# One decoder layer with 16 long contexts: a rewritten start, row-tiled self-attention scores, a split query spread and a last pair of its own

## The reference

```python
x = x + self_attention(layernorm(x), wq, wk, wv, wo)         # 32 query heads, 8 key heads of width 16, causal
x = x + cross_attention(layernorm(x), ctx, Wq_d, W_qk, Wkv_d, Wv_u)
x = x + ffn(layernorm(x), gate, kernel, bias, lora_A, lora_B, lora_As, lora_Bs)

# cross_attention, 16 heads, latent width 32
C_kv = ctx @ Wkv_d                                   # 1500 x 32 for each sequence
q    = (layernorm(x) @ Wq_d) @ W_qk                  # 56 x 16 x 32
out  = softmax(q . C_kv / sqrt(32)) @ (C_kv @ Wv_u)
# ffn
A_eff, B_eff = gate @ lora_A, gate @ lora_B          # one pair of factors for every two sequences
out  = x @ kernel + bias + (x @ A_eff.T) @ B_eff.T + (x @ lora_As.T) @ lora_Bs.T
```

## Time and profile before

| | |
|---|---|
| median of the runs | 679.4 us |
| profiled execution | 681.57 us, of which the span of instructions is 679.6 us |
| TensorE (PE) busy | 591.6 us, 87% |
| VectorE (DVE) | 442.2 us, 65% |
| GpSimd (POOL) | 424.9 us, 63% |
| ScalarE (ACT) | 303.8 us, 45% |
| chain that ended last | PE 62%, DVE 12%, issue 7%, POOL 6%, ACT 5%, SP queue 3%, DMA 3% |
| stages | prologue 64.7, body 0 68.8, bodies 1 to 6 73.6 each in the mean, body 7 62, body 8 and the store 42 us |

### The profile page before, as it was taken

One profiled execution on the slowest core, in us unless ns is written; L12 is line 12 of the kernel. 1 busy time (PEld: TensorE's weight loads), 2 busy tenths in 40 slices (PEclk: granted clock), 3 DMA queues, 4 the chain that ended last, 5 costly groups with the idle time before them and its releaser, 6 DMA issues.

```text
span 679.6 us, 12918 instructions
## 1 busy us (share of the span) xinstructions
PE 591.6 (87%) x3856; PEld 306.8 (45%) x3856; DVE 442.2 (65%) x717; ACT 303.8 (45%) x641; POOL 424.9 (63%) x394
## 2 busy tenths in 40 slices
...
GB/s 310 211 210 245 236 119 18 78 210 166 43 29 228 211 44 1 115 323 57 17 42 271 154 43 31 225 215 43 1 130 333 32 15 47 43 9 1 22 1 14
DMA packets 31410, 77.22 MB, mean 114 GB/s; under 512 B 11378, under 2 KB 25042, under 8 KB 28915
## 3 DMA queue, kind: packets, MB, share of 16 engines
...
...
## 4 chain that ended last, share of the span: by engine, by line
PE 62%; DVE 12%; issue 7%; POOL 6%; ACT 5%; SPq 3%; DMA 3%; POOLq 0%; ACTq 0%; DVEq 0%
PE st_ps L649 11%; PE mx_ps L677 10%; PE pv_ps L664 9%; POOL acc L1096 5%; PE mi_ps L459 4%; PE mi_ps L466 4%; PE mi_ps L453 4%; PE mi_ps L512 4%; SPq L371 3%; PE mi_ps L631 2%; DVE mx_p L1020 2%; DVE sm L982 2%; PE mi_ps L537 2%; DMA b_eff<-acc 2%; PE mi_ps L635 2%
## 5 line engine op out<-in xcount | busy, mean ns | idle before, releaser
L1096 POOL TENSOR_TENSOR acc<-acc,p_ring 125x448 f32<-125x448 f32 x300 | 359.8, 1199 | 49.2 <-ACT p_ring L833 23.5
L1020 DVE TENSOR_REDUCE mx_p<-mx_ps 128x1 f32<-128x500 f32 x336 | 210.7, 669 | 101.7 <-PE mx_ps L677 100.6
L833 ACT ACTIVATE p_ring<-st_ps 125x448 f32<-125x448 f32 x384 | 189.7, 544 | 171.4 <-PE st_ps L649 164.4
L649 PE MATMUL st_ps<-q_st,c_st 98*125 98x448 f32 x384 | 155.3, 432 | 13.4 <-ACT p_ring L833 7.7
L677 PE MATMUL mx_ps<-c_st,q_st 96*128 96x500 f32 x336 | 139.4, 446 | 14.9 <-DMA q_st<-q_hl 11.2
L649 PEld LDWEIGHTS st_ps<-q_st,c_st 98*125 98x125 f32 x384 | 68.7, 191 | 117.1 <-ACT p_ring L833 88.2
L1104 POOL TENSOR_TENSOR rstd<-mv,eps_col 128x1 f32<-128x1 f32 x24 | 4.6, 192 | 153.2 <-DVE mv L894 153.2
L664 PE MATMUL pv_ps<-p_ring,c_nat 125*32 125x448 f32 x768 | 94.4, 564 | 1.0 <-ACT p_ring L833 0.9
L677 PEld LDWEIGHTS mx_ps<-c_st,q_st 96*128 96x128 f32 x336 | 63.2, 196 | 41.4 <-issue 20.6
L1096 POOL TENSOR_TENSOR acc<-p_ring 125x448 f32<-125x448 f32 x30 | 36.6, 1221 | 27.3 <-ACT p_ring L833 27.3
L466 PE MATMUL mi_ps<-ctx_sb,wkv_sb 128*32 128x375 f32 x512 | 48.1, 496 | 0.7 <-DVE p L943 0.7
...
## 6 DMA issues: line engine op xcount, KB each, us to landing
...
```

The source lines that it names most:

```text
L649: mm(st_ps[unit % STB][0:KC, 0:HALF], c_st[:, b % 4, t * KT + k * KC:t * KT + (k + 1) * KC], q_st[:, b // 2 % 2, b % 2, half * HALF:(half ...
L833: act.activation(p_ring[:, unit % PR, :], st_ps[unit % STB][0:KC, 0:HALF], ACT.Exp, scale=float(L) ** -0.5).then_inc(exp_done, 1)
L1020: ve.tensor_reduce(mx_p[:, p:p + 1], mx_ps[unit % MXB][:, 0:KP], AX.X, ALU.max).then_inc(red_done, 1)
L1096: po.tensor_tensor(dst, first, p_ring[:, unit % PR, :].rearrange("p (h s) -> p h s", s=S), ALU.add).then_inc(acc_done, 1)
```

## The change

Five parts in one.

1. Prologue. The host pads `x` to 64 rows, so that no memset precedes its load and one DMA brings a pair. A dummy exponential loads ScalarE's table early; eight matmuls on the identity run ahead of the first transposes; GpSimd makes the masks before its first `power`. Keys' weights load first, the first context before the raw low-rank factors, the second context and pair before the cross weights. The raw factors lie in `kern_sb`, `ox` and `x3n` instead of the second context slot, and their eight matmuls are strewn between the steps (2, 1, 4, 1) instead of standing as 6 and 2. The first spread of queries comes right behind `H`, six DMAs from SP and six from ScalarE, ahead of the write of the factors; ScalarE waits for that write only before the first exponential.
2. Query spread by blocks. `q_in` is four semaphores, one for each block of 224 columns. SP issues blocks 0 and 1 behind `H`, and blocks 2 and 3 behind `MT` and its `spread_m`. A maxima piece waits only for the block that it reads.
3. Row-tiled self-attention scores. The keys are copied 4 times instead of 8; `SA` and `SB` take two `r` each, with the key groups 0 to 3 in array rows 0 to 63 (bank 0) and 4 to 7 in rows 64 to 127 (bank 1): 8 matmuls of 224 columns each instead of 4 of 448.
4. Orders. In group 3 the three pieces between the scores move in among `SA` and `SB`, and `NM` comes before `SB` is copied; `SN1` before `AS`; in group 9 one piece moves out of the scores and the pieces stand between `YT`, `T2`, `CQ` and `H`.
5. The end. VectorE adds the denominators of (sequence 14, half 1) and (15, 0), TensorE counts those of (15, 1) with matmuls on ones; the last sequence's scores use four banks; `DN` of the last pair goes ahead of `Y`, in a bank of the maxima; `fill` puts identity matmuls in four places.

```diff
-PIECES_IN = [3, 2, 4, 3, 0, 0, 0, 3, 4, 1, 3, 0]
+Q_BLOCKS = {0: (0,), 1: (1,), 3: (2,), 5: (3,)}
+PIECES_IN = [3, 2, 4, 0, 0, 0, 0, 3, 4, 0, 3, 0]
...
+LAST_STEPS = {6: ["XC"], 7: ["DN", "Y"], 8: ["DT"], 9: ["YT", "N2"], 10: ["T3"], 11: ["F1", "Fh", "F2"]}
+LAST_FILL = {"Y": 2, "YT": 2, "T3": 14, "F1": 2}
+DVE_HALVES = [(B - 2, 1), (B - 1, 0)]
+PE_HALF = (B - 1, 1)
...
+        def st_bank(unit):
+            if unit >= (B - 1) * 24:
+                return [*st_ps, *mx_ps[1:]][unit % 4]
+            return st_ps[unit % STB]
...
+            def spread_q(n, blocks):
+                sp.wait_ge(qh_hi, due(qh_hi, n + 1))
+                sp.wait_ge(qh_lo, due(qh_lo, n + 1))
+                for t in blocks:
+                    for part, dst in ((0, 0), (0, L), (1, 2 * L)):
                         dma(q_st[dst:dst + L, n % 2, :, t * 4 * S:(t + 1) * 4 * S].bitcast(F32),
+                            q_hl[t * L:(t + 1) * L, part, :, :].bitcast(F32)).then_inc(q_in[n % 2][t], 16)
...
-            sp.wait_ge(eff_out, due(eff_out, 32))
-            spread_q(0)
...
+            def fill(count):
+                for _ in range(count):
+                    mm(mx_ps[MXB - 1][:, 0:128], ident[:, :], ident[:, :], start=True, stop=True)
...
+                if name == "WA":
+                    pe.wait_ge(q1_sb, due(q1_sb, n + 1))
+                    pe.wait_ge(k_sb, due(k_sb, 2 * n + 2))
+                if name == "WB":
+                    pe.wait_ge(s1_sb, due(s1_sb, 4 * n + 2))
...
-                    for b in range(2):
-                        last = mm(o[b * SLOT:(b + 1) * SLOT, 0:G * S], qt[:, r, b * SLOT:(b + 1) * SLOT],
-                                  khat[:, b, :, :].rearrange("p g k -> p (g k)"), start=True, stop=True)
+                elif name in ("SA", "SB"):
+                    for j in range(2):
+                        r = 2 * (name == "SB") + j
+                        for half in range(2):
+                            rows = slice(half * 64, (half + 1) * 64)
+                            for b in range(2):
+                                last = mm(mi_ps[half][b * SLOT:(b + 1) * SLOT, j * 4 * S:(j + 1) * 4 * S],
+                                          qt[rows, r, b * SLOT:(b + 1) * SLOT],
+                                          khat[rows, b, :, :].rearrange("p g k -> p (g k)"), start=True, stop=True)
...
-                        pe.wait_ge(s1_sb, due(s1_sb, 2 * n + 3))
+                        pe.wait_ge(s1_sb, due(s1_sb, 2 * n + 4))
...
+            def last_counts(b, g):
+                half, k = g // KG, g % KG
+                pe.wait_ge(exp_done, due(exp_done, b * 24 + g * 4 + 4))
...
+                for u in range(4):
+                    ring = p_ring[:, (b * 24 + g * 4 + u) % PR, :].rearrange("p (q t s) -> p t q s", q=2, t=4)
+                    for t in range(4):
+                        cells = mx_ps[0][t * L:(t + 1) * L, :].rearrange("p (q b s) -> p q b s", q=4, b=2)
+                        mm(cells[:, half * 2:half * 2 + 2, 1, 0:S], ones[0:KC, :], ring[:, t, :, :],
+                           start=(k == 0 and u == 0), stop=(k == KG - 1 and u == 3))
...
+            def add_up(b, g):
...
+                for t in range(4):
...
+                    ve.tensor_tensor(dst, first, p_ring[:, unit % PR, :].rearrange("p (h s) -> p h s", s=S),
+                                     ALU.add).then_inc(acc_dve, 1)
```

Two of the changed lines of `STEPS`, groups 3 and 9:

```diff
-    [("M", 1), ("S0", "n"), ("S1", "n"), ("S2", "n"), ("S3", "n"), ("SM0", "n"), ("NM", "m"), ("SM1", "n")],
+    [("WA", "n"), ("M", 1), ("SA", "n"), ("M", 2), ("WB", "n"), ("M", 1), ("NM", "m"), ("SB", "n"), ("SM0", "n"),
+     ("SM1", "n")],
...
-    [("YT", "f"), ("T2", "n"), ("M", 2), ("CQ", "n"), ("H", "n"), ("N2", "f")],
+    [("YT", "f"), ("M", 1), ("T2", "n"), ("M", 1), ("CQ", "n"), ("M", 1), ("H", "n"), ("N2", "f")],
```

More of the change, by code:

```diff
@@ L103, in steps_of @@
 def steps_of(i, g):
+    if i == PAIRS:
+        for name in LAST_STEPS.get(g, []):
+            yield name, PAIRS - 1
+        return
     done = sum(PIECES_IN[g // GROUPS * GROUPS:g + 1])
```

282 lines of the change are left out of this document (175 added, 107 removed), and 1 row of the table STEPS.

## The result

The changed kernel takes 657.1 us (median of 4 runs, 656.01 to 659.25) against 679.3 for the kernel before on the same chip: a ratio of 0.968, 95% interval 0.965 to 0.971. Forecast were 652.5 us. The profiled execution is 656.01 us, its span 654.2.

What follows compares the result with a forecast made beforehand. It took a chain of differing limits: DMA latency in the prologue, VectorE and ScalarE within nearly full TensorE bodies, GpSimd's additions in body 7. Terms -15.5 - 3.6 + 2 - 4.1 - 6.0 = -27.2 gave 654.4 profiled, 652.5 against runs; range 640 to 666.

Steps and rivals of the forecast that it cites:

- Start: Prologue up to the first maxima piece: shorter chain and earlier query DMAs bring that piece to 49.2, -15.5 us.
- Rival C: Prologue: latents or queries queue behind the second context's DMAs; first piece at 54, 657.5 us in all; chance 0.09.
- `SN1` comes first now, -1.9: Body 0, VectorE: `SN1` no longer stands behind `AS`, its 0.97 us wait and 0.9 us length; -1.9 us.
- second step (maxima rows, -1.7): Body 0: six of twelve query DMAs come after the maxima rows' issue, taking 1.7 us off a 4.85 us wait.
- rival B: Bodies 1 to 6: new waits cool TensorE, one more clock dip each, 9 to 12 us; 661.5 to 664.5; chance 0.17.
- +0.35: Bodies 1 to 6: each gets 0.35 us longer through VectorE's chain, +2 us for the six.
- the chain of 10.0 to 10.4 us: Loop bodies, VectorE from first score copy to end of `SM1`: 10.0 to 10.4 us instead of 9.0, with three pieces inside.
- what row tiling gives TensorE is idle time here: Bodies 1 to 6: VectorE's chain sets the pace, so TensorE's time saved on scores becomes waits at `WB`, `Ah` and next scores.
- Rival A: Bodies 1 to 6: TensorE limits the loop after all; 2.8 us gained per body, 633.5 us in all; chance 0.10.
- Body 7: Additions moved to VectorE let GpSimd's `power` run at 621.5 and `T3` start earlier; -4.1 us.
- with four the exponentials set it, 2.1 us: Body 8: with four score banks the exponentials set a group's time, 2.1 us instead of 2.8 with two.
- Rival D: Self-attention scores: row tiles do not run side by side, 6.8 us for both calls; +32, 684.5 us; chance 0.03.

Runs made afterwards that it cites:

- as_first: The changed kernel with `AS` of the second sequence ahead of `SN1` again: 653.8 us, ratio 0.968.
- full_array: The changed kernel with row tiling undone, `SA` and `SB` as four matmuls of 448 columns over all 128 rows, orders kept: 665.4 us, ratio 0.982.
- pool_14: The changed kernel with the additions of (sequence 14, half 1) on GpSimd again: 662.8 us, ratio 0.977.
- late_sums: The changed kernel with the last sequence's context sums and counts behind a group's third score matmul instead of the second: 655.8 us, ratio 0.962.
- no_fill: The changed kernel without the identity matmuls of the end: 659.6 us, ratio 0.974.

## Why the prediction was right, and where it was not

The range and the sign held; the centre was 4.6 us low. Of that 1.6 are the terms and their rounding against the profiled execution (654.4 forecast, 656.01), 1.9 the correction to the median (the prediction says 2.2 and takes off 1.9), which the profiled execution of the new kernel does not share, and 1.1 that this execution lies under its own median.

That the terms add up so well is partly luck: up to the end of body 1 the forecast gained 4.4 us too much, and in bodies 2 to 7 3.9 us too little.

- **Start: right** (-15.5; measured -15.0 in this profile, -13.0 to -14.4 in the five with the same start), and in its split too: 7.9 us ahead of the queries' copy and 7.1 behind it. Rival C is out (first piece at 49.7, not 54).
- **Body 0: the step "`SN1` comes first now, -1.9" failed** (-3.6 for the body; measured -1.7). It has the opposite sign: by `as_first` the new place costs 0.9 us up to `O1`. Half of the -1.9 was never there. The prediction takes the 0.97 us at 95.31 of the earlier trace rows for a wait of VectorE, but VectorE was at work on `SN0` then, and `AS` followed at once, in the kernel before:

```profile
95.28 1.09 DVE L996 TENSOR_TENSOR p<-p,sm 128x896 f32<-128x896 f32 x1
96.29 0.35 DVE L921 CAST ct_hl<-ct_f 128x375 fp32r<-128x375 f32 x1
```

  The other half, 0.9 us of `AS`, becomes 2.7 in its new place, which I priced at nothing, although shows a subtraction of 1.61 and a cast of 0.81 beside GpSimd. The second step (maxima rows, -1.7) was somewhat too large: the wait is 3.66 instead of 4.85, -1.2.
- **Body 1: not forecast, and not shown to have changed.** The +2.4 is of this profile: five with the same code have 74.1 to 76.3 us, around the 74.9 before. What moves is how long TensorE stays at its low level behind the wait for the maxima rows, here some 9 us. That is not rival B, which has new waits cool TensorE: this wait is an old one, and shorter than before.
- **Bodies 2 to 6: sign wrong for the clean ones** (+0.35; measured -0.9 on bodies 2 and 6, -0.6 on body 4). The step that failed is the chain of 10.0 to 10.4 us. The start 0.7 us earlier came true (`SA` at 20.5 us behind the last `F2`, before 21.4); the chain grew by 0.27, not 1 or more, since one slow form falls in it, not two. `full_array` says that without row tiling the same orders would give +0.4, and so confirms the +0.35 only for a kernel without it: "what row tiling gives TensorE is idle time here" left out that its results come earlier, and the first copy with them (0.7 us). The forecast that TensorE would wait 1.0 us at `Ah` failed too; there is no such wait. Rival A is out: 1.2 us a body, not 2.8. Rival B is out as a rule: bodies 2 to 6 have a granted clock of 1.00.
- **The loop's branch: missed.** +0.3 and +0.6 on bodies 3 and 5, although the dip of the clock in body 3 (0.98 in the earlier trace rows) is gone. The issue wait of 1.1 us is new.
- **Body 7: right** (-4.1, measured -4.9), by `pool_14`.
- **Body 8: -6.0, measured -4.9.** From the first score to `Y` it is 20.4 us (616.88 to 637.28), not 19.25. The step that failed is "with four the exponentials set it, 2.1 us": I counted banks, and the sums' place between the second and third score set 2.42. `late_sums` shows it. `Y` to `YT` (1.9) and `T3` to the end (7.0) came out as forecast; of the latter 3.3 the identity matmuls gave 2.0 and cost 0.4 ahead; the other 1.3 came without them (`Fh` 2.69 against 3.78 before).
- **Rival D is out**: 0.99 us a call.

Open: why the bodies behind the branch lose another 1.3 to 2.7 us when `NM` stands late (0.9 of it is the slow subtraction of `SM1`), and what of the branch's 2.3 us is not the issue wait. Why the level came back sooner in `no_fill` than before the change was not tested.
